# Attention with layernorm: x turned by 32x32 blocks on VectorE in place of TensorE transposes

## The chip, the cores and the metric

One core of one Trainium2 chip runs the whole kernel. The time is that of the device in microseconds (us), lower is better.

## The reference

x is (16, 30, 30, 512) in float32: 16 images of S = 900 tokens with 512 features. Everything is float32; each image goes through 8 heads of 64:

```python
q, k, v = proj(wq, bq), proj(wk, bk), proj(wv, bv)          # (B, 8, 900, 64)
scores = einsum('bhqd,bhkd->bhqk', q, k) / sqrt(64) + bias   # bias by |dh| + |dw| on the 30 x 30 grid
ctx = einsum('bhqk,bhkd->bhqd', softmax(scores), v)
resid = ctx_as_tokens @ wo + bo + x
out = (resid - mean) * rsqrt(var + 1e-5) * gamma + beta
```

## The kernel before

**Units and slots.** An image's attention is 60 units: 4 pairs of heads by 15 units of two image rows of queries (60 queries, both heads; the keys in two halves lie on different partitions). The order of everything is written out by hand over the unit number u, and each engine runs its own `body(im, u)`. TensorE acts on even u alone. A slot (even u) on TensorE is: the scores of units u + 6 and u + 7 (L693, 32 matmuls), a part of the P·V product of one group of up to 4 units (L713, `PV_UNITS` at L44; 8 blocks, then 7), and background work in r_ps, two PSUM banks used in turn.

**Background work.** `SEQUENCE` (L82) lists the items: `piece` (p, j), a half of K or Q of pair p of heads (L610), `out` t, a tile of 120 tokens of the output projection of the image before (L653), `value` t, a tile of V (L628), and `xt` t. All but `xt` have KT = 4 steps of three matmuls (a float32 operand is split into a rounded high part and the rest, and three of the four products are added); an `xt` is one step. `room_at` (L90) says how many steps a slot may hold, and `place` (L105) fills the slots in sequence and gives each item the unit `EVICT` in which it leaves PSUM. It comes out as: out tiles leave at u = 5, 7, 7, 9, 13, 17, 19 and 23, `xt` steps stand in the slots 28, 30, 34, 36, 38, 40, 42 and 44, one value tile in each of 34 to 44, and 128 steps besides the eight `xt` steps in all.

**x of the next image.** `load_x` (L500) on SyncE's queue loads 120 tokens, a token per partition, into one of 4 slots of `tokens` (units in `LOAD_X`, L47, for the first four, then two units after an `xt`). `xt_tile` (L572) transposes it on TensorE, four 120x128 transposes into one bank (L585). `xt_hi` (L749) copies the bank rounded to float32r into `xt[:, 0]` on ScalarE (L752). `xt_lo` (L920) subtracts that from the bank on VectorE into `xt[:, 1]` (L924) and frees the bank. `piece` and `value_tile` (L593, L615) read both parts. The residual of the layernorm takes the same `tokens` slots (`load_residual`, L504).

**Softmax.** VectorE adds the bias and takes the row minimum (L939, `biased_scores(u + 6)`; it may begin when TensorE has written the unit's scores, and TensorE may write a unit's scores when VectorE is done with the unit two before). ScalarE takes the exponential with its sum (L809, u + 6). The two halves of the keys then exchange minimum and sum: `exchange` (L491) issues four DMAs of 1 KB on SyncE's queue (L497), GpSimd finds the difference (`leads`, L1033, line L1041), ScalarE its exponential (`ratios`, L817), GpSimd the weight (`totals`, L1043, line L1052), ScalarE scales the rows (`normalise`, L825, u + 2) and VectorE block-transposes them for P·V (`turn`, L944, line L952, unit u).

**Out tiles.** GpSimd splits the context (`split_context`, L1067 and L1069, units in `SPLIT_UNITS`) and adds bias to the residual (`add_bias`, L1079); VectorE adds, takes statistics and centres (`out_sum`, L955, lines L963 to L969) in the unit of `EVICT`, and scales two units later (`out_norm`, L972, line L977); SyncE stores. `keep_value` (L481) stores value tiles from ScalarE's copy, `load_values` reads them back.

Of the kernel before, what the change touches and what calls it, by code (L numbers as in the profile page):

```python
# [13 lines left out]
TT = 120  # L14
# [32 lines left out]
LOAD_X = [22, 22, 25, 28]  # L47
# [42 lines left out]
def room_at(u):  # L90

    if u in (2, 32):
        return 3
    if u == UNITS - 2:
        return 2
    if u == 30:
        return 2
    return 4 if u < 16 and u % 4 == 0 else 5


def steps(item):
    return 1 if item[0] in ("xt", "first_xt", "bv_wo") else KT


def place(items):  # L105

    at, ends, room, u = {}, {}, 0, 0
    for item in items:
# [8 lines left out]
        ends[item] = min(e + (1 if used <= 2 or item[0] in ("xt", "out") else 2), UNITS - 1)  # L117
# [5 lines left out]
XT_UNITS = [u for tile in range(NT) for u in STEPS for w in STEPS[u] if w[0] == xt(tile)]  # L123
# [148 lines left out]
def attention_layernorm(nc, x, wq, bq, wk, bk, wv, bv, wo, bo, gamma, beta, spatial_bias, out):  # L272
# [3 lines left out]
    with ExitStack() as ctx:  # L276
# [31 lines left out]
        tokens = sb("tokens", [TT, SLOTS, D])  # L308
# [86 lines left out]
        xt_hi_done = sem("xt_hi_done")  # L395
# [42 lines left out]
        def _(sp):  # L438
# [75 lines left out]
            def body(im, u):  # L514
# [18 lines left out]
                if not im.last:  # L533
                    for t in range(SLOTS):
# [30 lines left out]
        def _(pe):  # L565
# [6 lines left out]
            def xt_tile(im, t):  # L572

                use = (im.xt, t)
                bank = bank_of(use)
                bank_wait(im, use)
                if isinstance(im, Prologue):
# [569 lines left out]
```

## Time and profile before

| | us |
|---|---|
| median of 3 runs | 3302.53 (3301.56 to 3307.05) |
| the profiled execution, its own time | 3300.92 |
| its span, first to last instruction | 3299.0 |
| TensorE busy | 3141.2 |
| ScalarE busy | 2758.5 |
| VectorE busy | 2608.9 |
| GpSimd busy | 1413.7 |

The sum, below, is made against the profiled execution. Names in the rows: PE is TensorE, PEld its weight loads, DVE VectorE, ACT ScalarE, POOL GpSimd, SPq SyncE's queue; L610 is line 610 of the kernel; xN is a count. In a row of windows stand the stretch and its length in us, then busy us and instructions of each engine, the granted TensorE clock (1.00 is full speed), the mean busy share of the 16 DMA engines and GB/s. In a row of the groups by line stand names, shapes and count, then busy us and mean ns of one, then the idle time of the engine before them and what ended it.

### The profile page before, as it was taken

How to read it: one execution, taken by the hardware profiler on the slowest of the kernel's cores; microseconds unless marked ns; L12 is line 12 of the kernel's file. 1: busy time of each engine (PE TensorE's matmuls, PEld its weight loads, DVE VectorE, ACT ScalarE, POOL GpSimd, SP SyncE). 2: the span in 40 equal slices, each digit the busy share in tenths (PEclk: the TensorE clock that was granted, in tenths of full speed). 3: DMA queues.
4: the chain of work that ended last, by engine and by line, in shares of the span. 5: the costliest groups of instructions: out<-in, count | busy, mean ns of one | idle time of the engine just before them, and what ended most of it. 6: DMA issues, size and time to landing. Idle time of an engine off the chain costs nothing. (4 is left out here: it accounts for less than half of the span.)

```text
span 3299.0 us, 127110 instructions
## 1 busy us (share of the span) xinstructions
PE 3141.2 (95%) x52744; PEld 2127.7 (64%) x52744; DVE 2608.9 (79%) x5589; ACT 2758.5 (84%) x7015; POOL 1413.7 (43%) x3049
## 2 busy tenths in 40 slices
PE   2899999999999999999999999999999999999986
PEld 2566666666666666666666666666666666666654
DVE  2477978878797887979778797887979778797887
ACT  1698897988889898898988889898898988889784
POOL 0133536354262533526344262543526344262545
PEclk7999999999999999999999999999999999999999
DMA  5222322323223232322323223232322323223221
GB/s 159 62 78 72 96 72 73 99 61 96 83 78 90 68 95 70 95 71 73 99 60 95 83 79 90 66 93 73 96 70 74 99 60 96 84 78 90 66 74 27
DMA packets 317939, 267.44 MB, mean 81 GB/s; under 512 B 109913, under 2 KB 240985, under 8 KB 317361
## 3 DMA queue, kind: packets, MB, share of 16 engines
q1 hardware_dynamic: 172242, 130.32, 15.2%
q10 hardware_dynamic: 145120, 129.00, 13.3%
q8 instruction: 415, 6.80, 0.9%
q14 instruction: 162, 1.33, 0.1%
HBM read 193.73 MB, written 63.66 MB: 78 GB/s over the span
## 5 line engine op out<-in xcount | busy, mean ns | idle before, releaser
L939 DVE CUSTOM_DVE_ANT_0 prob<-s_ps,window 128x450 f32<-128x450 f32 x1920 | 1108.3, 613 | 458.9 <-PE s_ps L693 458.8
L809 ACT ACTIVATE prob<-prob,own 128x450 f32<-128x450 f32 x1920 | 1266.2, 663 | 161.0 <-DVE own L939 151.0
L825 ACT ACTIVATE prob<-prob,weight 128x450 f32<-128x450 f32 x1920 | 1173.3, 660 | 75.0 <-POOL weight L1052 75.0
L952 DVE STREAM_TRANSPOSE prob_t<-prob 128x960 f32<-128x960 f32 x960 | 1125.5, 1173 | 57.4 <-PE pv_ps L713 34.5
L713 PEld LDWEIGHTS pv_ps<-prob_t,values 64*64 64x64 f32 x30720 | 752.5, 133 | 379.3 <-issue 335.8
L693 PE MATMUL s_ps<-k_sb,q_sb 64*32 64x450 f32 x15360 | 845.9, 544 | 43.8 <-DVE own L939 42.1
L713 PE MATMUL pv_ps<-prob_t,values 64*64 64x120 f32 x30720 | 856.2, 260 | 26.3 <-ACT ctx_sb L835 24.2
L610 PE MATMUL r_ps<-xt,w_sb 128*128 128x450 f32 x3072 | 705.8, 377 | 9.0 <-ACT stage L783 3.9
L610 PEld LDWEIGHTS r_ps<-xt,w_sb 128*128 128x128 f32 x3072 | 562.1, 189 | 94.7 <-issue 29.4
L1038 POOL TENSOR_TENSOR lead<-own,other 128x4 f32<-128x4 f32 x480 | 112.1, 233 | 1017.2 <-DMA other<-own 1016.8
L1052 POOL TENSOR_TENSOR weight<-total,minus_one 128x4 f32<-128x4 f32 x480 | 503.0, 1048 | 37.7
L693 PEld LDWEIGHTS s_ps<-k_sb,q_sb 64*32 64x32 f32 x15360 | 227.8, 106 | 436.8 <-issue 333.5
L628 PE MATMUL r_ps<-wv_sb,xt 128*120 128x512 f32 (+1 forms) x1536 | 391.5, 402 | 41.9 <-DVE wv_sb L908 38.6
L653 PE MATMUL r_ps<-wo_sb,ctx_split 128*120 128x512 f32 x1536 | 396.6, 403 | 4.6 <-POOL ctx_split L1069 3.3
L1047 POOL TENSOR_TENSOR total<-ratio,other 128x4 f32<-128x4 f32 x480 | 106.0, 221 | 661.2 <-ACT ratio L817 633.0
L809 ACT ACTIVATION_READ_ACCUMULATOR prob<-prob,own 128x1 f32 x1920 | 365.8, 191 | 0.0
L628 PEld LDWEIGHTS r_ps<-wv_sb,xt 128*120 128x120 f32 (+1 forms) x1536 | 261.1, 176 | 120.8 <-issue 41.3
L653 PEld LDWEIGHTS r_ps<-wo_sb,ctx_split 128*120 128x120 f32 x1536 | 271.3, 182 | 84.9 <-issue 17.6
L1079 POOL TENSOR_TENSOR tokens<-tokens,bo_all 120x512 f32<-120x512 f32 x120 | 156.3, 1308 | 56.9 <-DMA tokens<-in_x 56.9
L939 DVE DVE_READ_ACCUMULATOR2_ANT own<- 128x1 f32 x1920 | 157.3, 82 | 0.0
L1069 POOL TENSOR_TENSOR ctx_split<-ctx_sb,ctx_split 128x480 fp32r<-128x480 f32 (+1 forms) x128 | 149.9, 1171 | 10.3
L817 ACT ACTIVATE ratio<-lead 128x4 f32<-128x4 f32 x480 | 94.7, 197 | 67.5 <-POOL lead L1041 65.0
(56 smaller groups left out, 1462.7 us busy)
## 6 DMA issues: line engine op xcount, KB each, us to landing
w_sb<-w_split ACTq DMA_DIRECT2D x126, 512.0 KB, 4.0
values<-v_dram ACTq DMA_DIRECT2D x256, 240.0 KB, 3.2
tokens<-in_x SPq DMA_DIRECT2D x214, 240.0 KB, 3.2
other<-own SPq DMA_DIRECT2D x1920, 1.0 KB, 2.2
out<-tokens SPq DMA_DIRECT2D x105, 240.0 KB, 2.7
v_dram<-stage SPq DMA_DIRECT2D x96, 240.0 KB, 2.8
v_dram<-stage SPq DMA_DIRECT2D x32, 180.0 KB, 2.4
tokens<-in_x SPq DMA_DIRECT2D x30, 120.0 KB, 3.4
```

The lines of the kernel that those rows point to most:

```text
L610: last = pe.matmul(r_ps[:, bank, 0:HALF], w_sb[:, kind, a, k, :], xt[:, c, k, columns(half)], start=(k == 0 and i == 0), stop=(k == KT - 1 ...
L628: last = pe.matmul(r_ps[0:n, bank, :], xt[:, a, k, at:at + n], wv_sb[:, c, k, :], start=(k == 0 and i == 0), stop=(k == KT - 1 and i == PA ...
L653: last = pe.matmul(r_ps[0:TT, bank, :], ctx_split[:, t % 2, a, k, :], wo_sb[:, c, k, :], start=(k == 0 and i == 0), stop=(k == PAIRS - 1 a ...
L693: last = pe.matmul(s_ps[row:row + QUAD, u % 2, head, 0:HALF], q_sb[d, p % 2, q0:q0 + QUAD], k_sb[d, p % 2, columns(r)], start=True, stop=T ...
L713: last = pe.matmul(pv_ps[d, a, 0:n * GRID].rearrange("d (u w) -> d u w", u=n), values[half, p % 2, j, d], prob_t[half, g % 2, 0:n, head, Q ...
L809: nc.scalar.activation(prob[:, im.unit(u) % RING, head, 0:HALF], prob[:, im.unit(u) % RING, head, 0:HALF], ACT.Exp, scale=-1.0, bias=own[: ...
L825: nc.scalar.activation(prob[:, im.unit(u) % RING, head, 0:HALF], prob[:, im.unit(u) % RING, head, 0:HALF], ACT.Copy, scale=weight[:, s, c: ...
L939: nc.vector.tensor_tensor_reduce(prob[:, im.unit(u) % RING, head, 0:HALF], s_ps[:, u % 2, head, 0:HALF], window[:, w0:w0 + HALF // GRID, : ...
L952: nc.vector.transpose(out=prob_t[:, g % 2, v % PER_GROUP, :, :].rearrange("p h k -> p (h k)"), in_=prob[:, im.unit(u) % RING, :, :].rearra ...
L1052: nc.gpsimd.tensor_tensor(weight[:, s, :], total[:, s, :], minus_one[:, :], ALU.pow).then_inc(weight_done, 1)
L1069: nc.gpsimd.tensor_tensor(ctx_split[:, t % 2, 1, :, 0:m], src, ctx_split[:, t % 2, 0, :, 0:m].bitcast(F32), ALU.subtract).then_inc(split_l ...
L1079: nc.gpsimd.tensor_tensor(y, y, bo_all[0:rows(t), :], ALU.add).then_inc(res_bias, 1)
```

## The change

x of the next image is loaded in tiles of 128 tokens (`X_TILES` = 8, the last of 4 tokens), by four DMAs each, one for every 32 features of each group of 128. Each puts 32 tokens on 32 partitions, so that VectorE's block transpose of the whole tile (`turn_x`) gives features on partitions and tokens along the row. ScalarE writes the rounded part into `xt` (`x_split_hi`) and GpSimd the rest (`x_split_lo`). The `xt` items leave `SEQUENCE`, `room_at` is written anew, and value tiles and pieces wait for GpSimd's `x_lo`. The first image still passes TensorE. By the planner the out tiles now leave at u = 5, 7, 9, 11, 13, 17, 21 and 25; the slots 4 to 16 hold 4, 4, 4, 5, 4, 5, 4 steps (before 4, 5, 4, 5, 4, 5, 5), 24 to 34 hold 4, 5, 4, 4, 3, 5, and 36 to 44 a value tile each. `X_UNITS` is 31, 33, 35, 37, 39, 41, 43, 44.

```diff
-LOAD_X = [22, 22, 25, 28]
+LOAD_X = [22, 24, 28, 32]
...
-SEQUENCE += [xt(0), xt(1)]
-for tile in range(NT - 2):
-    SEQUENCE += [value(tile), xt(tile + 2)]
-SEQUENCE += [value(NT - 2)] + pieces(4) + [value(NT - 1)] + pieces(5, (0, 1, 2))
+SEQUENCE += [value(tile) for tile in range(NT - 1)] + pieces(4) + [value(NT - 1)] + pieces(5, (0, 1, 2))
...
 def room_at(u):
-    if u in (2, 32):
+    if u in (2, 32, UNITS - 2):
         return 3
-    if u == UNITS - 2:
-        return 2
-    if u == 30:
-        return 2
-    return 4 if u < 16 and u % 4 == 0 else 5
+    return 5 if u in (10, 14, 18, 22, 26, 34, 46, 48, 50, 52, 54) else 4
...
+VALUE_UNITS = [min(u for u in STEPS for w in STEPS[u] if w[0] == value(tile)) for tile in range(NT)]
+X_UNITS = [u - 1 for u in VALUE_UNITS[:NT - 1]]
+X_UNITS += [X_UNITS[-1] + 1]
...
+        x_turned = sb("x_turned", [128, 2, D])
...
             def load_x(b, t):
-                sp.dma_start(x_nat[0:rows(t), t % SLOTS, :], x_t[b, t * TT:t * TT + rows(t), :]
-                             ).then_inc(x_in[t % SLOTS], 16)
+                n = x_rows(t)
+                blocks, m = -(-n // QUAD), min(QUAD, n)
+                for a in range(128 // QUAD):
+                    part = bass.AP(tensor=x.tensor, offset=x.offset + (b * S + XB * t) * D + QUAD * a,
+                                   ap=[[D, m], [128, KT], [QUAD * D, blocks], [1, QUAD]])
+                    sp.dma_start(x_nat[QUAD * a:QUAD * a + m, t % SLOTS, 0:KT * blocks * QUAD].rearrange(
+                        "p (k b c) -> p k b c", k=KT, b=blocks), part).then_inc(x_in[t % SLOTS], 16)
...
-                        if u == XT_UNITS[t] + 2:
-                            use = ("xt", t)
-                            sp.wait_ge(bank_full[bank_of(use)], im.use(use) + 1)
+                        if u == X_UNITS[t]:
+                            sp.wait_ge(x_turn, X_TILES * im.b + t + 1)
                             load_x(im.b + 1, t + SLOTS)
...
+                    if j == 0 and p == PAIRS and im is not pro:
+                        pe.wait_ge(x_lo, X_TILES * (im.b + 1))
...
-                        xt_ready(im, t)
+                        pe.wait_ge(x_lo, X_TILES * im.b + x_tiles_to(at + n))
...
+            def x_split_hi(im, t):
+                n, m = X_TILES * im.b + t, x_rows(t)
+                if t == 0:
+                    for use in pieces(PAIRS - 1, (2, 3)):
+                        act.wait_ge(bank_full[bank_of(use)], im.use(use) + 1)
+                act.wait_ge(x_turn, n + 1)
+                turned_x = x_turned[:, t % 2, 0:KT * QUAD * -(-m // QUAD)].rearrange("p (k t) -> p k t", k=KT)[:, :, 0:m]
+                nc.scalar.activation(xt[:, 0, :, XB * t:XB * t + m], turned_x, ACT.Copy).then_inc(x_hi, 1)
...
+                for t in range(X_TILES):
+                    if X_UNITS[t] == u and not im.last:
+                        x_split_hi(im, t)
...
+            def turn_x(im, t):
+                n, width = X_TILES * im.b + t, KT * QUAD * -(-x_rows(t) // QUAD)
+                dve.wait_ge(x_in[t % SLOTS], 64 * (X_TILES // SLOTS * im.b + t // SLOTS + 1))
+                if n >= 2:
+                    dve.wait_ge(x_lo, n - 1)
+                nc.vector.transpose(out=x_turned[:, t % 2, 0:width], in_=x_nat[:, t % SLOTS, 0:width]).then_inc(x_turn, 1)
...
+                for t in range(X_TILES):
+                    if X_UNITS[t] - 2 == u and not im.last:
+                        turn_x(im, t)
...
+            def x_split_lo(im, t):
+                n, m = X_TILES * im.b + t, x_rows(t)
+                turned_x = x_turned[:, t % 2, 0:KT * QUAD * -(-m // QUAD)].rearrange("p (k t) -> p k t", k=KT)[:, :, 0:m]
+                pool.wait_ge(x_hi, n + 1)
+                nc.gpsimd.tensor_tensor(xt[:, 1, :, XB * t:XB * t + m], turned_x,
+                                        xt[:, 0, :, XB * t:XB * t + m].bitcast(F32), ALU.subtract).then_inc(x_lo, 1)
...
+                for t in range(X_TILES):
+                    if X_UNITS[t] == u and not im.last:
+                        x_split_lo(im, t)
```

`x_split_hi` stands in ScalarE's body behind the evictions and ahead of the exponentials, `turn_x` behind `turn` in VectorE's, `x_split_lo` in GpSimd's behind `totals` or `leads` and `reciprocal_std`.

## Rows read from the trace of the kernel before

**Rows 1.** The page: span; busy time, share and instructions of each engine.
```profile
span 3299.0 us, 127110 instructions
...
PE 3141.2 (95%) x52744; PEld 2127.7 (64%) x52744; DVE 2608.9 (79%) x5589; ACT 2758.5 (84%) x7015; POOL 1413.7 (43%) x3049
```

**Rows 2.** Windows, image 7, slots u = 4, 6, 10, 12, 24, 28, 30, 38, 58.
```profile
1507.62:1514.17 6.55, 6.53 (x109) 4.26 (x108) 5.42 (x12) 6.55 (x19) 4.21 (x8) 1.00 0.09 27
1514.17:1521.10 6.93, 6.93 (x104) 4.57 (x104) 6.83 (x15) 5.44 (x16) 6.53 (x12) 1.00 0.15 40
...
1527.54:1534.96 7.42, 6.84 (x104) 4.52 (x103) 7.32 (x17) 4.62 (x13) 6.25 (x13) 1.00 0.26 69
1534.96:1542.87 7.91, 6.67 (x110) 4.13 (x109) 7.91 (x17) 6.54 (x19) 4.34 (x6) 1.00 0.21 65
1576.22:1582.96 6.74, 6.74 (x112) 4.87 (x111) 6.17 (x14) 5.87 (x17) 2.96 (x7) 1.00 0.54 146
1589.49:1596.04 6.55, 6.55 (x113) 4.79 (x112) 4.43 (x10) 4.19 (x10) 1.86 (x5) 1.00 0.42 117
1596.04:1601.07 5.03, 4.59 (x96) 2.76 (x96) 3.30 (x7) 4.92 (x14) 1.43 (x3) 1.00 0.57 154
...
1621.25:1628.03 6.78, 6.78 (x113) 4.32 (x112) 5.09 (x11) 6.66 (x19) 2.07 (x6) 1.00 0.42 113
...
1689.03:1693.91 4.88, 4.88 (x103) 3.18 (x102) 3.79 (x10) 4.88 (x14) 1.42 (x3) 1.00 0.55 163
```

**Rows 3.** Timeline of VectorE in those slots: start, us, engine, line, operation.
```profile
1508.72 0.63 DVE L939 CUSTOM_DVE_ANT_0 prob<-s_ps,window 128x450 f32<-128x450 f32 x1 [1.42 <-PE s_ps L693]
...
1511.98 1.17 DVE L952 STREAM_TRANSPOSE prob_t<-prob 128x960 f32<-128x960 f32 x1
1513.08 0.65 DVE L963 TENSOR_TENSOR tokens<-r_ps,tokens 120x512 f32<-120x512 f32 x1
...
1515.41 0.61 DVE L939 CUSTOM_DVE_ANT_0 prob<-s_ps,window 128x450 f32<-128x450 f32 x1
...
1521.39 1.41 DVE L969 SCALAR_TENSOR_TENSOR tokens<-tokens,mean_var,gamma_all 120x512 f32<-120x512 f32 x1
...
1525.05 0.74 DVE L977 SCALAR_TENSOR_TENSOR tokens<-tokens,rstd,beta_all 120x512 f32<-120x512 f32 x1
1525.71 0.62 DVE L939 CUSTOM_DVE_ANT_0 prob<-s_ps,window 128x450 f32<-128x450 f32 x1
```

**Rows 4.** Timeline of TensorE: its waits in u = 10 and u = 12.
```profile
1529.11 0.99 PE L693 MATMUL s_ps<-k_sb,q_sb 64*32 64x450 f32 x16 [0.58 <-DVE own L939]
...
1537.08 0.99 PE L693 MATMUL s_ps<-k_sb,q_sb 64*32 64x450 f32 x16 [1.14 <-DVE own L939]
```

**Rows 5.** Groups of instructions by line, whole run.
```profile
L952 DVE STREAM_TRANSPOSE prob_t<-prob 128x960 f32<-128x960 f32 x960 | 1125.5, 1173 | 57.4 <-PE pv_ps L713 34.5 <-ACT prob L825 22.8
...
L1069 POOL TENSOR_TENSOR ctx_split<-ctx_sb,ctx_split 128x480 fp32r<-128x480 f32 (+1 forms) x128 | 149.9, 1171 | 10.3
...
L924 DVE TENSOR_TENSOR xt<-r_ps,xt 128x480 fp32r<-128x480 f32 (+1 forms) x128 | 77.6, 608 | 49.0 <-ACT xt L752 48.6
...
L752 ACT ACTIVATE xt<-r_ps 128x480 fp32r<-128x480 f32 (+1 forms) x128 | 67.5, 528 | 38.0 <-PE r_ps L585 38.0
...
L747 ACT ACTIVATE w_sb<-prob 128x512 fp32r<-128x512 f32 x2 | 1.3, 630 | 13.8 <-DMA prob<-in_L_conv_wq 9.4 <-DMA prob<-in_L_conv_wk 4.4
```

**Rows 6.** Waits, 1600 to 1800 us: us in total, times, longest us.
```profile
ACT ratio L817 <- POOL lead L1041: 3.1, 5, 1.1
...
PE r_ps L585 <- ACT q_sb L765: 0.9, 2, 0.4
```

**Rows 7.** DMA queues, 44 to 56 us, only the copy into `bias_by_w` under way.
```profile
q1 hardware_dynamic: 758, 0.09, 10.5%
```

**Rows 8.** Source view of the exchange's DMAs, L497.
```profile
DMA to landing us min/median/max: 1.6/2.2/4.5
```

**Rows 9.** Timeline of SyncE: four DMAs of one exchange.
```profile
1598.05 2.42 SPq L497 DMA_DIRECT2D other<-own  x4
```

More of the change, by code:

```diff
@@ L116, in place @@
         e = u - 2
-        ends[item] = min(e + (1 if used <= 2 or item[0] in ("xt", "out") else 2), UNITS - 1)
+        ends[item] = min(e + (1 if used <= 2 or item[0] == "out" else 2), UNITS - 1)
     assert max(at) < UNITS
@@ L122 @@
 STEPS, EVICT = place(SEQUENCE)
-XT_UNITS = [u for tile in range(NT) for u in STEPS for w in STEPS[u] if w[0] == xt(tile)]
+XB = 128
+X_BLOCKS = XB // QUAD
+X_TILES = -(-S // XB)
+VALUE_UNITS = [min(u for u in STEPS for w in STEPS[u] if w[0] == value(tile)) for tile in range(NT)]
+X_UNITS = [u - 1 for u in VALUE_UNITS[:NT - 1]]
+X_UNITS += [X_UNITS[-1] + 1]
+assert X_UNITS[0] > max(u for u in STEPS for w in STEPS[u] if w[0] == ("piece", PAIRS - 1, 3))
 BANK = {item: n % 2 for n, item in enumerate(SEQUENCE)}
@@ L142, in wanted @@
         return not first
-    if item[0] in ("xt", "value") or item[0] == "piece" and item[1] >= PAIRS:
+    if item[0] == "value" or item[0] == "piece" and item[1] >= PAIRS:
         return not last
@@ L260, in rows, with x_rows, x_tiles_to @@
     return LAST if t == NT - 1 else TT
+def x_rows(t):
+    return min(XB, S - XB * t)
+def x_tiles_to(token):
+    return -(-token // XB)
 def value_rows(t):
@@ L394, in attention_layernorm @@
         bank_free = [sem(f"bank_free{i}") for i in range(BANKS)]
-        xt_hi_done = sem("xt_hi_done")
+        first_hi = sem("first_hi")
+        x_turn = sem("x_turn")
+        x_hi = sem("x_hi")
+        x_lo = sem("x_lo")
         first_x_in = [sem(f"first_x_in{t}") for t in range(NT)]
@@ L570, in bank_wait, with first_xt @@
                     pe.wait_ge(bank_free[bank], n)
[L572 to L577, printed above, removed]
-                    tile = first_x(t)
-                    pe.wait_ge(first_x_in[t], 16)
-                else:
-                    tile = x_nat[:, t % SLOTS, :]
-                    pe.wait_ge(x_in[t % SLOTS], 16 * (NT // SLOTS * im.b + t // SLOTS + 1))
-                n = rows(t) if isinstance(im, Prologue) else TT
+            def first_xt(t):
+                use = ("first_xt", t)
+                bank, tile, n = bank_of(use), first_x(t), rows(t)
+                bank_wait(pro, use)
+                pe.wait_ge(first_x_in[t], 16)
                 for k in range(KT):
@@ L658, in work_on @@
             def work_on(im, work, k0=0, k1=KT):
-                if work[0] in ("xt", "first_xt"):
-                    xt_tile(im, work[1])
+                if work[0] == "first_xt":
+                    first_xt(work[1])
                 elif work[0] == "piece":
@@ L747, in weight_hi, with first_hi_of @@
                 nc.scalar.activation(dst, src, ACT.Copy, scale=scale).then_inc(w_hi, 1)
-            def xt_hi(im, t):
-                m, bank = rows(t), bank_of((im.xt, t))
-                act.wait_ge(bank_full[bank], im.use((im.xt, t)) + 1)
+            def first_hi_of(t):
+                m, bank = rows(t), bank_of(("first_xt", t))
+                act.wait_ge(bank_full[bank], pro.use(("first_xt", t)) + 1)
                 nc.scalar.activation(xt[:, 0, :, t * TT:t * TT + m],
                                      r_ps[:, bank, 0:KT * TT].rearrange("p (k t) -> p k t", k=KT)[:, :, 0:m],
-                                     ACT.Copy).then_inc(xt_hi_done, 1)
+                                     ACT.Copy).then_inc(first_hi, 1)
+            def x_split_hi(im, t):
[6 more added lines that the diff above has]
+                nc.scalar.activation(xt[:, 0, :, XB * t:XB * t + m], turned_x, ACT.Copy).then_inc(x_hi, 1)
             def keep_piece(im, p, j):
@@ L843, in _ @@
             for t in range(NT):
-                xt_hi(pro, t)
+                first_hi_of(t)
             weight_hi(wk_split[:, 0], raw_wk)
@@ L856, in body @@
                 for work in im.evicted(u):
-                    if work[0] == "xt":
-                        xt_hi(im, work[1])
-                    elif work[0] == "piece":
+                    if work[0] == "piece":
                         keep_piece(im, *work[1:])
@@ L1012, in body @@
                 for work in im.evicted(u):
-                    if work[0] == "xt":
-                        xt_lo(im, work[1])
-                    elif work[0] in ("out", "final"):
+                    if work[0] in ("out", "final"):
                         out_sum(im, work)
```

33 lines of the change are left out of this document (14 added, 19 removed).

## The prediction

> **What bounds the kernel now.** I read the page's engine table first: over the span TensorE is busy 95%, more than any other engine [rows 1]. A mean over stages settles nothing, so I then cut one middle image, b = 7, where the scores of a new pair of units start on TensorE (the even u of the plan). Each stretch is then one slot of the hand-written order: scores of two units, one part of a P·V group, 2 to 5 background steps. In the slots u = 24, 28, 38 and 58 TensorE's busy time equals the stretch and its clock is 1.00, that is 2.4 GHz [rows 2]: there the time is TensorE's own work. Two places differ. In u = 10 and 12 TensorE is idle 0.6 and 1.2 us while VectorE is busy for 7.32 of 7.42 and all of 7.91 us: the stage where the output tiles of the image before are normalised is VectorE's. In u = 30 TensorE is idle 0.44 us. ScalarE is a close second in the value stage: 6.66 of 6.78 us in u = 38 [rows 2].
>
> **TensorE: what goes.** Eight slots per image hold an `xt` step of four transposes. Slots alike in their P·V part (8 blocks of 4 units) price the steps: u = 24 has five piece steps in 6.74 us, u = 58 two in 4.88, so a piece step is 0.62; u = 28 has four and an `xt` in 6.55, so the `xt` is 6.55 - 6.74 + 0.62 = 0.43. u = 4 (four out steps, 6.55) gives 0.62 + 0.43 / 4 = 0.73 for an out step, u = 38 (four value steps and an `xt`, 6.78) 0.68 for a value step; scores and 8 blocks are 4.88 - 1.24 = 3.64. All 128 other steps stay, so 8 x 0.43 = **3.4 us per image** goes from the engine that sets the pace, provided no other wait takes the place.
>
> **The new order of the out tiles.** Rooms of 4 in place of 5 move the DVE evictions from u = 5, 7, 7, 9, 13 to 5, 7, 9, 11, 13. VectorE's own times: it starts a slot's body 1.10 us after TensorE's (1507.62 to 1508.72), two units' scores and turns take 4.36 (1508.72 to 1513.08), an out tile 2.33 (1513.08 to 1515.41), and its last operation, two units later, 0.66 (1525.05 to 1525.71) [rows 2, 3]. TensorE's second unit of scores starts 0.9 us into a slot (16 matmuls take 0.99 to their modelled end [rows 4]), but needs VectorE to be 3.27 us into the body before (1508.72 to 1511.98). With two tiles in one body this fails: the waits on VectorE of 0.58 and 1.14 us are that [rows 4], and the two slots together stand 7.42 + 7.91 - 6.5 - 6.45 = 2.4 us above what their steps come to by the prices above. After, counted from the start of u = 4: TensorE's slots start at 6.5, 12.7, 19.3, 25.8, 32.4, 38.9 (3.64 for scores and 8 P·V blocks, 3.3 with 7 by u = 6, plus steps). VectorE takes 4.36 + 2.33 + 0.66 = 7.35 per body and starts them at 7.8, 15.1, 22.5, 29.8, 37.2. It falls behind 1 us per slot, and first holds TensorE at u = 16: 37.2 + 3.27 = 40.5 against 38.9 + 0.9 = 39.8, a wait of 0.7. Some of its SCALAR_TENSOR_TENSORs are stretched, 1.41 us at 1521.39 against 0.74 at 1525.05 [rows 3]; at 0.3 us more per tile the same sum gives 1.9. I take 1.2, so of the 2.4 **1.1 us per image**, rounded down, comes back here (bounds 0.4 and 1.6). After u = 16 the bodies hold at most one tile every second slot and VectorE catches up.
>
> The Trainium skill (SBUF — State Buffer, "SBUF: two separate sides") says that a VectorE operation with two SBUF inputs and a GpSimd operation take turns on a shared port pair, for a whole instruction. The stretched row agrees. By that rule, with GpSimd's work spread evenly over these slots, many more could be held; the third rival below has its price from rows.
>
> **u = 30.** TensorE's idle 0.44 us and waits of 0.9 us per image at the transposes for ScalarE's bank [rows 2, 6] fall with the step; its slot is filled with four pieces (5.9 us). I take **0.5** (bounds 0 and 0.7).
>
> **ScalarE.** Eight copies from PSUM of 528 ns become seven of 128x512 from SBUF and a small one; the nearest row is 630 ns [rows 5], so 7 x 0.63 + 0.2 - 8 x 0.53 = +0.4 us per image. In the value slots its demand stays about 6.4 to 6.6 where TensorE's falls to 6.2 to 6.4 (7.0 in u = 34, which gets five steps). So the two tie. ScalarE works ahead: VectorE waited for its scaled rows 22.8 us in 960 turns [rows 5]. The copy of block 0 also waits for piece (3, 3), to the end of u = 30.
>
> **VectorE.** Eight subtracts of 608 ns become seven block transposes of 512 columns. 960 columns take 1173 ns [rows 5]; 512 lie between 0.63 (in proportion) and 0.75 (with 0.2 us fixed). 4.9 us out, 4.6 to 5.5 in: nothing, hidden by VectorE being busy only 5.1 of 6.8 us in these slots [rows 2]. Without that cover it would cost at most 0.6 us. x block 3 is the tight one: SyncE issues it at u = 32 behind block 4 and an exchange, for a turn at u = 35; I count a landing 0 to 1 us late, inside the 3 us that VectorE may lag before TensorE notices.
>
> **GpSimd.** The subtract of 128x480 takes 1171 ns [rows 5], so 128x512 some 1.25, seven times, 9 us per image beside 2.1 busy of 6.8 [rows 2]. It stands in odd bodies between `leads` and `totals`. ScalarE meanwhile runs two exponentials of 0.66 and the ratio, so `totals` is late by 0 to 1 us and the first scaling with it. A value tile needs the low part only a slot later.
>
> **DMA and SyncE.** Eight loads of 2 KB rows become 32 DMAs of 128 B runs, 14,400 packets per image. The nearest row is the prologue's copy of 120 B runs: 758 packets in 12 us at 10.5% of 16 engines, 0.105 x 16 x 12 / 758 = 26.6 ns of an engine each [rows 7]. A block of 2048 is 3.4 us of all 16 beside the latency, 24 us per image: some 12% more share. The loads are waited for 3 to 7 units after issue. What matters is who stands behind them: `exchange` uses the same queue, lands in 1.6 to 4.5 us, median 2.2 [rows 8], and the ratio already waits at times for what it feeds, 3.1 us in 200 [rows 6]. Four exchanges occupy SyncE 2.42 us [rows 9], 0.6 each, so a block's four loads 1.3 to 2.4. In odd units the exchange goes first and the next is two units off, so I charge the exchange, the late `totals` and ScalarE's tie together **0.4 us per image** (bounds 0 and 3).
>
> The skill (DMA: Bandwidth & Descriptors, "Rules for kernel authors") warns against many small transfers, mostly overhead under 64 KB; each new DMA has just 64 KB. By it the fourfold count is itself a price. That is the fourth rival's ground, and the trace has no load of this kind into SBUF.
>
> **Sum.** 3.4 + 1.1 + 0.5 - 0.4 = 4.6 us per image, 15 images with a next one to load (and 15 with out tiles): 69 us. The profiled execution took 3300.9 (a span of 3299.0 [rows 1] and 1.9 around it), which gives 3231.9; the median of the runs shown is 1.6 higher, so **3234 us**.
>
> **Rivals.**
> 1. ScalarE takes over in the value stage. For it: 6.66 busy of 6.78. Then the six `xt` steps of u = 34 to 44 are worth nothing (2.6 us) and the gain is 2.0 x 15 = 30 us: 3272. Against it: the lead it has. 0.14.
> 2. More than I sum: VectorE's stage runs with the wait of 0.7, nothing is charged for the chain, and u = 30 gives all: 3.4 + 1.6 + 0.7 = 5.7, 86 us, 3216. 0.20.
> 3. Port turns: if both SCALAR_TENSOR_TENSORs of each tile are held 0.6 us, a body is 8.5 us, starts are 16.3, 24.9, 33.4, 42, and TensorE waits about 5 us in place of 2.4. Gain 3.4 + 0.5 - 2.6 - 0.4 = 0.9, 13 us: 3289. Against it: GpSimd is busy 6.53 and 6.25 us in u = 6 and 10 already [rows 2], and the bodies there come to little over the sum of unstretched parts. 0.06.
> 4. Slower: the exchange. If the block loads push each of the eight exchanges near them to the 4.5 us landing, 2.3 later, and SyncE's longer issue adds 0.7, and the ratio has 1 us to spare, ScalarE stands 2 us eight times, 16 us, of which its lead takes some 9: 7 us against the 5.0 of the gains, so 2.0 x 15 = +30 us, 3332. It decides from 0.6 us per exchange on. For it: packet count and shared queue; against: the order in SyncE. 0.09.
> 5. The freed time only changes its name, TensorE waiting for `xt`'s low part where it transposed: 3302, 0.03.
>
> My forecast has 0.48. The range 3210 to 3280 takes in it, rival 1 and most of rival 2. A difference of 0.2% (6.6 us) is about what a measurement can tell. Faster 0.88 (the forecast and rivals 1 to 3), same 0.03, slower 0.09.
>
> **What would show it.** The transposes of L585 are left for the first image alone; slots u = 36 and 40 take 6.0 to 6.2 us and 38 and 42 near 6.4, with TensorE never idle (if ScalarE is busy all the slot and TensorE idle, rival 1). Waits of TensorE for VectorE's `own` near u = 14 and 16 only, about 1 us. The x transpose at 0.63 to 0.75 us. Landing of the exchanges still 2.2 in the median and ScalarE's wait for `lead` under 10 us in 200; more would be rival 4. TensorE waiting for GpSimd's low part of `xt` more than 0.5 us per image would prove my slack wrong.

## The result, and the profile after

| | before | after |
|---|---|---|
| median of 20 runs each, us | 3301.86 (3298.03 to 3307.05) | 3295.17 (3282.03 to 3301.57) |
| ratio, 95% interval | | 0.9976 (0.9968 to 0.9984) |
| span of the profiled execution | 3299.0 | 3295.8 |
| TensorE busy | 3141.2 | 3110.7 |

The kernel is faster by 0.24%, 6.7 us. The forecast was 3234 us with a range from 3210 to 3280, so it was wrong: about nine tenths of the expected gain is missing. This is the page after, its span, its engine table and the first DMA queue; the first two answer to [rows 1]:

```profile
span 3295.8 us, 126643 instructions
...
PE 3110.7 (94%) x52264; PEld 2090.6 (63%) x52264; DVE 2613.4 (79%) x5589; ACT 2760.8 (84%) x7015; POOL 1553.7 (47%) x3169
...
q1 hardware_dynamic: 379902, 130.34, 18.0%
```

TensorE has 30.5 us less work and the span is only 3.2 us shorter: TensorE now waits where it did not. To find where, I added up the slots of all middle images (1 to 13) from the timeline of TensorE, each from one start of scores to the next. Means per image in us, by stretches of the plan:

| slots u | before | after | one DMA per tile (below) |
|---|---|---|---|
| 0 to 2 | 12.46 | 12.44 | 12.45 |
| 4 to 14 | 42.34 | 40.83 | 40.60 |
| 16 to 28 | 46.49 | 45.09 | 45.11 |
| 30, 32 | 11.81 | 12.37 | 12.37 |
| 34 to 44 | 40.25 | **42.67** | 38.71 |
| 46 to 54 | 32.86 | 32.86 | 32.86 |
| 56, 58 | 11.74 | 11.66 | 11.69 |
| sum | 197.96 | 197.92 | 193.78 |

Some steps have also moved between stretches: by the planner u = 4 to 14 hold 26 steps and no longer 27, u = 16 to 28 hold 31 (before 34), u = 30 and 32 hold 7 (before 4), and u = 34 to 44 hold 25 (before 24), so a stretch alone does not give the worth of one part of the change. Up to u = 32 the image gains 2.4 us; the value stage, u = 34 to 44, takes back the same 2.4, and stands 4.0 above what it takes with one DMA per tile. Two slots do it: u = 36 is 7.25 in the mean and u = 40 is 8.86, both widely scattered (standard deviations of 1.3 and 1.6 us), where the last column has 6.23 and 6.24. These are u = 36, 38, 40 and 42 of image 7 after, in the view of windows (busy us and count of each engine, TensorE's clock, DMA share, GB/s):

```profile
1612.11:1619.40 7.29, 6.28 (x101) 4.02 (x100) 5.63 (x12) 5.33 (x14) 3.04 (x6) 1.00 0.37 71
1619.40:1625.80 6.40, 6.40 (x110) 3.93 (x109) 5.03 (x11) 3.48 (x10) 3.10 (x6) 1.00 0.57 120
1625.80:1635.87 10.07, 7.45 (x102) 4.65 (x101) 5.20 (x11) 9.15 (x23) 3.54 (x8) 0.87 0.27 65
1635.87:1642.68 6.81, 6.81 (x109) 4.25 (x108) 4.63 (x11) 6.69 (x18) 2.72 (x4) 0.94 0.31 94
```

TensorE idles 1.0 us in u = 36 and 2.6 in u = 40. In u = 38 nothing is lost on TensorE, but ScalarE is busy for only 3.48 of 6.40 us, in a stage that should keep it full: its stop there is what TensorE pays for a slot later. The waits of TensorE in the whole profiled execution, after (line waited for: us, times, longest), and the groups of the lines that stand between SyncE and it (the first three with the shapes kept apart, so without the 15 short tiles of 4 tokens):

```profile
PE r_ps L632 <- POOL xt L1101: 43.6, 27, 3.6
...
PE s_ps L697 <- DVE own L962: 31.8, 51, 1.5
```

```profile
L950 DVE STREAM_TRANSPOSE x_turned<-tokens 128x512 f32<-128x512 f32 x105 | 71.0, 676 | 22.9 <-DMA tokens<-in_x 22.9
...
L768 ACT ACTIVATE xt<-x_turned 128x512 fp32r<-128x512 f32 x105 | 65.0, 619 | 8.6 <-issue 6.6
...
L1101 POOL TENSOR_TENSOR xt<-x_turned,xt 128x512 fp32r<-128x512 f32 x105 | 134.6, 1282 | 57.4 <-ACT xt L768 56.8
...
L797 ACT ACTIVATE stage<-r_ps 120x512 f32<-120x512 f32 (+1 forms) x128 | 74.3, 580 | 57.0 <-DMA v_dram<-stage 47.7 <-PE r_ps L632 9.1 <-ACT stage L797 0.2
...
L831 ACT ACTIVATE ratio<-lead 128x4 f32<-128x4 f32 x480 | 94.5, 197 | 109.2 <-POOL lead L1065 108.0
```

The last two in the kernel before:

```profile
L783 ACT ACTIVATE stage<-r_ps 120x512 f32<-120x512 f32 (+1 forms) x128 | 74.4, 582 | 15.5 <-PE r_ps L628 15.3 <-ACT stage L783 0.2
...
L817 ACT ACTIVATE ratio<-lead 128x4 f32<-128x4 f32 x480 | 94.7, 197 | 67.5 <-POOL lead L1041 65.0
```

TensorE's value tile (L632) waits 43.6 us for GpSimd's rest of x, 2.9 per image. The engines on the way wait as well: VectorE's block transpose 22.9 us for its load, GpSimd 56.8 for ScalarE's rounded part (this one is no sign by itself: with one DMA per tile, below, it is still 44.1 and TensorE does not wait), and ScalarE 47.7 us for a **store**, `v_dram<-stage`, the transfer out of its own staging buffer. That wait was not there in the kernel before: the same group (L783) waited 15.5 us, 15.3 of it for TensorE. The ratio's wait for `lead` went from 65.0 to 108.0. The durations themselves are near what was expected: 676 ns for a whole tile's block transpose, 619 for its rounded part, 1282 for its rest.

Loads, stores and exchanges have one thing in common, SyncE's queue. Its timeline in the same image (start, duration, line, names, how many in a row):

```profile
1600.91 3.13 SPq L501 DMA_DIRECT2D other<-own  x4
1604.09 6.72 SPq L511 DMA_DIRECT2D tokens<-in_x  x8
1610.86 2.53 SPq L501 DMA_DIRECT2D other<-own  x4
1613.43 2.67 SPq L511 DMA_DIRECT2D tokens<-in_x  x4
1616.14 2.53 SPq L501 DMA_DIRECT2D other<-own  x4
1618.72 2.67 SPq L511 DMA_DIRECT2D tokens<-in_x  x4
1621.49 0.56 SPq L493 DMA_DIRECT2D v_dram<-stage  x1
1622.10 3.44 SPq L501 DMA_DIRECT2D other<-own  x4
1625.65 0.52 SPq L493 DMA_DIRECT2D v_dram<-stage  x1
1626.21 2.76 SPq L511 DMA_DIRECT2D tokens<-in_x  x4
```

From 1604.09 to 1629 the queue has no gap over 0.11 us. There are two jams in it. **First**, tile 4 (u = 31) and tile 3 (u = 32) stand back to back, eight DMAs, 6.72 us; the exchange behind them starts at 1610.86, 3.8 us after the exponentials that it waits for had ended on ScalarE (1607.09). In the mean of the images 1 to 13 this exchange, of unit 38, goes out 3.0 us late and the next 2.4, where the kernel before has 0.0 for both. **Second**, the loads of the next tile (1618.72) stand ahead of the store at 1621.49, for whose landing ScalarE's next copy into that buffer waits. The other end of both, GpSimd and ScalarE in the same stretch:

```profile
1614.56 0.20 POOL L1062 TENSOR_TENSOR lead<-own,other 128x4 f32<-128x4 f32 x1 [5.71 <-DMA other<-own]
...
1615.04 1.27 POOL L1101 TENSOR_TENSOR xt<-x_turned,xt 128x512 fp32r<-128x512 f32 x1
...
1630.34 1.27 POOL L1101 TENSOR_TENSOR xt<-x_turned,xt 128x512 fp32r<-128x512 f32 x1 [2.62 <-ACT xt L768]
```

```profile
1626.48 0.60 ACT L797 ACTIVATE stage<-r_ps 120x512 f32<-120x512 f32 x1 [3.60 <-DMA v_dram<-stage]
...
1629.64 0.61 ACT L768 ACTIVATE xt<-x_turned 128x512 fp32r<-128x512 f32 x1
```

```profile
1616.46 3.02 PE L632 MATMUL r_ps<-wv_sb,xt 128*120 128x512 f32 x12 [1.01 <-POOL xt L1101]
...
1631.75 4.18 PE L632 MATMUL r_ps<-wv_sb,xt 128*120 128x512 f32 x12 [2.62 <-POOL xt L1101]
```

GpSimd's subtract stands behind `lead` in its program. `lead` waits 5.71 us for the late exchange, the subtract ends at 1616.31, and TensorE starts 1.01 us late. In the second jam ScalarE stands 3.60 us for the store, its rounded part starts at 1629.64, GpSimd's rest at 1630.34, and TensorE goes on 2.62 us late. That value tile then takes 4.18 us where the one before took 3.02, with the granted clock at 0.87 in the mean of the slot, so partly at 1.2 in place of 2.4 GHz: here the wait costs 1.2 us more after it has ended (7.45 busy, against 6.24 in the same slot without the wait, shown below).

Two theories stood at this point. **A**: SyncE's issue time, four DMAs of 0.64 us in place of one of 0.55, holds exchanges and stores. **B**: the 128 B runs themselves (379,902 packets on the queue, 172,242 in the kernel before) slow what lands beside them. Further suspects were GpSimd's long subtract, the place of the single loads, and the new order of the out tiles.

### The profile page after: what moved, and what is told of

It reads as the page before. It is cut to its first block and busy times, and to the rows that moved or that the text cites. A ratio compares the mean times of both kernels' runs of the same rounds, so it can differ in the third digit from the quotient of the medians.

```text
span 3295.8 us, 126643 instructions
## 1 busy us (share of the span) xinstructions
PE 3110.7 (94%) x52264; PEld 2090.6 (63%) x52264; DVE 2613.4 (79%) x5589; ACT 2760.8 (84%) x7015; POOL 1553.7 (47%) x3169
## 3 DMA queue, kind: packets, MB, share of 16 engines
q1 hardware_dynamic: 379902, 130.34, 18.0%
## 5 line engine op out<-in xcount | busy, mean ns | idle before, releaser
L697 PE MATMUL s_ps<-k_sb,q_sb 64*32 64x450 f32 x15360 | 850.1, 544 | 35.7 <-DVE own L962 31.8
L1062 POOL TENSOR_TENSOR lead<-own,other 128x4 f32<-128x4 f32 x480 | 101.7, 212 | 1098.2 <-DMA other<-own 1097.9
L632 PE MATMUL r_ps<-wv_sb,xt 128*120 128x512 f32 (+1 forms) x1536 | 400.7, 412 | 82.9 <-POOL xt L1101 43.6
L632 PEld LDWEIGHTS r_ps<-wv_sb,xt 128*120 128x120 f32 (+1 forms) x1536 | 270.8, 182 | 180.4 <-issue 100.6
L831 ACT ACTIVATE ratio<-lead 128x4 f32<-128x4 f32 x480 | 94.5, 197 | 109.2 <-POOL lead L1065 108.0
L1101 POOL TENSOR_TENSOR xt<-x_turned,xt 128x512 fp32r<-128x512 f32 x120 | 137.9, 1150 | 62.0 <-ACT xt L768 61.4
```

The source lines that it names most:

```text
L632: last = pe.matmul(r_ps[0:n, bank, :], xt[:, a, k, at:at + n], wv_sb[:, c, k, :], start=(k == 0 and i == 0), stop=(k == KT - 1 and i == PA ...
L697: last = pe.matmul(s_ps[row:row + QUAD, u % 2, head, 0:HALF], q_sb[d, p % 2, q0:q0 + QUAD], k_sb[d, p % 2, columns(r)], start=True, stop=T ...
L1101: nc.gpsimd.tensor_tensor(xt[:, 1, :, XB * t:XB * t + m], turned_x, xt[:, 0, :, XB * t:XB * t + m].bitcast(F32), ALU.subtract).then_inc(x_ ...
```

## The experiments

Every ratio is to the kernel before; a difference in us to the changed kernel is to its 3295.2.

### The same runs in one DMA, and plain rows

```diff
-                for a in range(128 // QUAD):
-                    part = bass.AP(tensor=x.tensor, offset=x.offset + (b * S + XB * t) * D + QUAD * a,
-                                   ap=[[D, m], [128, KT], [QUAD * D, blocks], [1, QUAD]])
...
+                token = XB * t if n < QUAD else min(XB * t, S - 224)
+                part = bass.AP(tensor=x.tensor, offset=x.offset + (b * S + token) * D,
+                               ap=[[D, m], [128, KT], [QUAD * D, blocks], [1, QUAD]])
```

> The changed kernel, but each x tile of 128 tokens is fetched by one DMA of 128 partitions with the same 2048 runs of 128 B, in place of four of 32 partitions. The parts of x land in other places than needed, so the sum of products is of other numbers; work and bytes are the same. Theory A (SyncE's issues: four loads of 0.67 us at each of u = 31, 32, 33, 35 and 37 push the exchange and the stores of the value tiles back): the slots u = 34 to 44 fall from 42.7 us per image to 39 to 39.5, and the time to 3235 to 3250. Theory B (the packets: 128 B runs slow the queue and the exchange): all packets are still there, so the time stays at 3290 to 3300. Theory C (GpSimd's subtract stands before the totals, ScalarE is the bound of the value slots): no change either, 3290 to 3300, and issue-to-exponential delays stay.

Measured: **3232.57 us, ratio 0.9797 (0.9782 to 0.9811)**. The packets stay (373,962 on the queue), the count of DMAs per tile falls from four to one of 0.68 us, and 63 us come off. Its groups:

```profile
L797 ACT ACTIVATE stage<-r_ps 120x512 f32<-120x512 f32 (+1 forms) x128 | 74.3, 580 | 18.4 <-DMA v_dram<-stage 9.5 <-PE r_ps L632 8.6 <-ACT stage L797 0.2
...
L950 DVE STREAM_TRANSPOSE x_turned<-tokens 128x512 f32<-128x512 f32 x120 | 74.6, 622 | 2.1 <-DMA tokens<-in_x 2.1
```

The wait for the store falls from 47.7 to 9.5, that of the transpose from 22.9 to 2.1, TensorE's for the rest of x is gone, and no exchange of the stage goes out late (0.0 in the mean for units 36 to 44).

```diff
+                m = x_rows(t)
+                width = D if m == 128 else KT * QUAD
+                sp.dma_start(x_nat[0:m, t % SLOTS, 0:width], x_t[b, XB * t:XB * t + m, 0:width]).then_inc(x_in[t % SLOTS], 16)
```

> The changed kernel with each x tile fetched by one DMA of 128 rows of 2 KB (the layout for the block transpose is left out, so values and pieces are made of x in another order). Neither four issues nor short runs. Theory A: the same time as with one DMA of 128 B runs, 3235 to 3250. Theory B: clearly faster than that one, by its 26.6 ns x 14,400 packets of engine time or more, and the first of the two that leaves 3290. Theory C: 3290 to 3300 still.

Measured: 3235.34 us, 0.9804 (0.979 to 0.9819). Sixteen times fewer packets per tile make no difference in time to the kernel with 128 B runs in one DMA, so B falls as the cause. The short runs do slow a neighbour a little: the store of the first value tile, which stands right behind a load, lands 4.2 us after its issue in the one kernel and 3.2 in the other (means over 15 images, by the trace; 4.4 in the changed kernel). ScalarE waits 9.5 us in all for that store in the one kernel and not at all in the other, and TensorE for it in neither.

### Four DMAs again, with runs of 512 B; and rows with three or five small DMAs

```diff
-                                   ap=[[D, m], [128, KT], [QUAD * D, blocks], [1, QUAD]])
+                                   ap=[[D, m], [QUAD * D, blocks], [1, 128]])
```

> The changed kernel with each of a tile's four DMAs fetching 4 runs of 512 B per partition (128 neighbouring features) in place of 16 runs of 128 B; same bytes, places and count of DMAs, a quarter of the packets (the order of the features in xt is then another than the weights', so the result is of other products). Theory A, an issue costs the same however long its runs: 3288 to 3300. If the issue time hangs on the pattern (three dimensions in place of four) and falls from 0.64 to near 0.35, as for the row loads: 3240 to 3260. Theory B: 3240 to 3260 too, but with issues still of 0.64 us.

Measured: 3239.4 us, 0.981 (0.9794 to 0.9827). This looks like B at first, since the count of DMAs stays and the packets fall. But the issue times moved too, as the view of one line shows (min/median/max ns):

```profile
L511 SPq DMA_DIRECT2D tokens<-in_x x480: 288/432/1903, 187.9 to 2957.4; - x160
```

In the changed kernel, the same line:

```profile
L511 SPq DMA_DIRECT2D tokens<-in_x x480: 583/637/1964, 189.0 to 3017.1; - x160
```

So a tile costs SyncE 1.7 us here and 2.5 to 2.8 there. To hold the two apart, the next two kernels load rows and add small DMAs of 1 KB each that only take up the queue.

```diff
+                for a in range(3):
+                    sp.dma_start(spare[:, t % SLOTS, 8 * a:8 * a + 8], x_t[b, QUAD * a:QUAD * a + QUAD, 0:8]).then_inc(x_in[t % SLOTS], 16)
```

> The version with one DMA of 2 KB rows per tile (3235 us), plus three DMAs per tile of 32 partitions x 32 B into a buffer that nobody reads: the issues come back, the bytes and short runs do not (96 packets a tile). The layout for the block transpose is left out as there. Theory A (SyncE's issue time alone): some 0.6 us each, 24 more per image at the same places, so the slots 34 to 44 go back to 42 to 43 us and the time to 3285 to 3300. Theory B (packets, DMA share): stays within 5 us of 3235.

Measured: 3238.67 us, 0.9805 (0.9791 to 0.982), against my expectation. The reason is in the issue times, which I had not measured for so small a DMA:

```profile
L511 SPq DMA_DIRECT2D spare<-in_x x360: 310/422/2238, 189.7 to 2958.0; - x180
```

Three at 0.42 and the rows at 0.58 are 1.8 us per tile: the count of four was back, SyncE's time was not. With five small ones:

> As the version with 2 KB rows and three small DMAs per tile (3239 us, where a tile took SyncE 0.58 + 1.36 = 1.9 us and not the 2.7 of the changed kernel: the small ones cost 0.42 each), but with five small ones: 0.58 + 5 x 0.45 = 2.8 us per tile. Nothing else of the changed kernel's loads is there (160 tiny runs a tile, one load of rows). Theory A, SyncE's time per tile at these places is the cause, whatever it is spent on: slots 34 to 44 back to 42 to 43.5 us, time 3285 to 3305. Rival: it takes the 128 B runs and four issues together (theory B in a mixed form): within 10 us of 3239.

Measured: **3295.73 us, 0.9983 (0.9972 to 0.9995)**: 0.58 + 5 x 0.42 = 2.7 us per tile, rows of 2 KB, and the whole loss is back. Its timeline of SyncE has the same first jam, now of twelve DMAs, and its groups the same waits:

```profile
1606.10 0.58 SPq L509 DMA_DIRECT2D tokens<-in_x  x1
1606.72 2.28 SPq L511 DMA_DIRECT2D spare<-in_x  x5
1609.05 0.42 SPq L509 DMA_DIRECT2D tokens<-in_x  x1
1609.52 3.08 SPq L511 DMA_DIRECT2D spare<-in_x  x5
1612.64 2.41 SPq L502 DMA_DIRECT2D other<-own  x4
```

```profile
L796 ACT ACTIVATE stage<-r_ps 120x512 f32<-120x512 f32 (+1 forms) x128 | 74.4, 581 | 49.5 <-DMA v_dram<-stage 40.2 <-PE r_ps L631 9.2 <-ACT stage L796 0.2
```

A is shown: SyncE's time per tile decides, whatever the DMAs carry. The exchanges of units 38 and 40 are late again too, by 3.6 and 3.3 us in the mean. The dose is sharp: 1.8 us per tile costs 3 to 6 us in all against one DMA (3238.7 to 3235.3 and 3232.6, about what the measurement can tell), 2.7 costs 60.

### Which jam: tile 3 earlier, the store first, both

```diff
-LOAD_X = [22, 24, 28, 32]
+LOAD_X = [22, 24, 28, 30]
```

> The changed kernel with the load of x tile 3 issued at u = 30 in place of u = 32, nothing else; the result is whole. In the trace SyncE idles some 4 us there, while at u = 31 and 32 eight loads in a row take 6.72 us and the next exchange is issued 3.1 us after its exponential. Theory A: the exchange of unit 38 goes out within 0.5 us of its exponential, the slots 34 to 44 lose 1.5 to 3 us per image, time 3250 to 3275. Theories B and C: same packets, same subtract, no change, 3290 to 3300.

Measured: 3266.55 us, 0.9897 (0.9883 to 0.9912), 29 us under the changed kernel. Slot 36 is whole again (6.23 in the mean over images), slot 40 is not (7.93). The exchange of unit 38 is not within the 0.5 us of the expectation, it is still 1.1 us late in the mean (3.0 in the changed kernel). ScalarE still waits for the store:

```profile
L797 ACT ACTIVATE stage<-r_ps 120x512 f32<-120x512 f32 (+1 forms) x128 | 74.3, 580 | 51.4 <-DMA v_dram<-stage 43.1 <-PE r_ps L632 8.1 <-ACT stage L797 0.2
```

The other jam alone: tiles 4 to 7 are issued at u = 31, 33, 36 and 38, so that tiles 6 and 7 follow the stores of their slots, and tile 3 stays at 32.

```diff
+MORE_X = [31, 33, 36, 38]
...
-                        if u == X_UNITS[t]:
+                        if u == MORE_X[t]:
```

> The changed kernel with tiles 6 and 7 loaded at u = 36 and 38, behind the stores of value tiles, and tile 3 left at u = 32 behind tile 4. It splits the gain of the version with all three moved (3235.5) from the other side: tile 3 alone gave 29 us (3266.5). If the two jams are separate, the store's share is the other 31 us and this stands at 3262 to 3270. If the late exchange of unit 38 feeds the later one, this wins little: 3275 to 3290.

Measured: 3252.68 us, 0.9857 (0.9842 to 0.9872), 42 us under. Slot 40 falls to 6.59, slot 36 stays at 7.42. ScalarE's wait for the store is gone (1.4), while the exchanges of units 38 and 40 stay 3.4 and 2.8 us late and VectorE still waits for its load:

```profile
L798 ACT ACTIVATE stage<-r_ps 120x512 f32<-120x512 f32 (+1 forms) x128 | 74.2, 580 | 12.7 <-PE r_ps L633 11.1 <-DMA v_dram<-stage 1.4 <-ACT stage L798 0.2
...
L951 DVE STREAM_TRANSPOSE x_turned<-tokens 128x512 f32<-128x512 f32 x120 | 75.3, 627 | 28.2 <-DMA tokens<-in_x 26.4 <-POOL xt L1102 1.8
```

Both edits together, with all four 128 B loads per tile as in the change:

> The changed kernel, result whole, with only the places of its loads moved: tile 3 at u = 30 (was 32), tile 6 at u = 36 behind the store of the first value tile (was 35, ahead of it), tile 7 at 38 (was 37). Theory A: what is left of the loss with tile 3 moved alone (slot 40 at 7.9 us) is the store of a value tile that stands behind four loads, while ScalarE needs its staging buffer; with the store first, slot 40 falls to 6.3 to 6.8 and the time to 3235 to 3250. Theory B or C: 3260 to 3270 as with tile 3 alone.

Measured: **3235.51 us, 0.9798 (0.9777 to 0.9819)**. The change itself is worth 66 us, once two lists of units say when its loads are issued. It beats both kernels. The slots u = 36, 38, 40 and 42 of image 7 in this kernel, and SyncE in the first two of them:

```profile
1587.62:1593.84 6.22, 6.22 (x101) 4.02 (x100) 5.03 (x11) 6.10 (x16) 3.45 (x8) 1.00 0.57 115
1593.84:1600.24 6.40, 6.40 (x110) 3.93 (x109) 5.03 (x11) 6.28 (x17) 2.72 (x4) 1.00 0.49 91
1600.24:1606.48 6.24, 6.24 (x102) 4.03 (x101) 5.03 (x11) 6.12 (x16) 3.25 (x7) 1.00 0.36 92
1606.48:1612.93 6.45, 6.45 (x109) 4.23 (x108) 4.63 (x11) 6.33 (x17) 2.97 (x6) 1.00 0.41 111
```

```profile
1589.30 2.46 SPq L502 DMA_DIRECT2D other<-own  x4
1591.87 0.52 SPq L494 DMA_DIRECT2D v_dram<-stage  x1
1592.43 2.69 SPq L512 DMA_DIRECT2D tokens<-in_x  x4
1595.74 3.41 SPq L502 DMA_DIRECT2D other<-own  x4
```

TensorE is busy for the whole of every slot, at full clock. SyncE is as full in u = 36 as in a slot of the changed kernel with a load and a store, 2.5 + 0.5 + 2.7 = 5.7 of 6.2 us, but nothing urgent stands behind a load. The two jams are not a plain sum: by the medians their removal alone gives 29 and 42 us, together 60; in the profiled executions it is 33, 37 and 65, so which jam is the larger is not clear. One thing that both share is seen in the traces: an image in which TensorE's granted clock fell below 0.95 in a slot of the stage occurs 9 times in 15 in the changed kernel, 2 times with tile 3 moved, once with the store first and never with both. Whether that is all of the overlap is not shown.

### GpSimd's subtract, and the order of the out tiles

With the loads spread, the subtract is moved to VectorE, in the same units:

```diff
-                nc.gpsimd.tensor_tensor(xt[:, 1, :, XB * t:XB * t + m], turned_x,
+                nc.vector.tensor_tensor(xt[:, 1, :, XB * t:XB * t + m], turned_x,
                                         xt[:, 0, :, XB * t:XB * t + m].bitcast(F32), ALU.subtract).then_inc(x_lo, 1)
```

> The version with the loads spread, and the subtract that makes the rest of x moved from GpSimd to VectorE, in the same units, result whole. If GpSimd's place between leads and totals costs anything (theory C), this is faster than the loads spread alone, by up to 0.5 us per image. If not, VectorE's 0.65 us and its wait for ScalarE's rounded part come on top in slots where it is idle 1.5 us or more: 0 to +15 us over the loads spread alone.

Measured: 3238.65 us, 0.9813 (0.9795 to 0.983), the same as with GpSimd within the spread (3229 to 3244 there, 3238 to 3248 here). With the loads spread, GpSimd's 1285 ns for a whole tile are hidden as well as VectorE's 685, and the place of the subtract costs nothing. In the changed kernel itself the subtract stands behind the late `lead` on GpSimd and carries the first jam to TensorE; whether another place would have spared it there was not run.

The new plan of u below 28 is taken back to that of before, with u = 28 at four steps and u = 30 empty:

```diff
 def room_at(u):
-    if u in (2, 32, UNITS - 2):
+    if u < 28:
+        return 3 if u == 2 else 4 if u < 16 and u % 4 == 0 else 5
+    if u == 28:
+        return 4
+    if u == 30:
+        return 0
+    if u in (32, UNITS - 2):
```

> The changed kernel with the slots below u = 28 filled as in the kernel before (out tiles leave at 5, 7, 7, 9, 13, 17, 19, 23), u = 28 with piece (3, 3) and u = 30 with no step; the value slots unchanged. My reading of the VectorE stage: u = 4 to 14 goes back from 40.8 to 42.3 us per image, u = 30 becomes a short slot of about 5 us and the total is 1 to 2 us per image longer, 3305 to 3325. Rival: the order of the out tiles is worth nothing, since VectorE catches up later anyway: within 5 us of 3295.

Measured: 3317.66 us, 1.005 (1.0033 to 1.0067), 22.5 us over the changed kernel. TensorE's waits for VectorE's scores in it:

```profile
PE s_ps L703 <- DVE own L968: 63.6, 59, 1.5
```

They are 63.6 us, against 31.8 with the new order and 42.1 before. That looks like a large gain of the new order, and it is not: this kernel changes a second thing, the empty u = 30. Summed by slot over the images 1 to 13, TensorE waits for VectorE's scores 2.05 us per image in u = 8 to 12 (before 2.13) and another 1.53 in u = 32, right behind the empty slot, as in image 7:

```profile
1608.88 0.99 PE L703 MATMUL s_ps<-k_sb,q_sb 64*32 64x450 f32 x16 [1.53 <-DVE own L968]
```

The slot u = 30 is over in 3.27 us, and VectorE has not taken the scores that TensorE must overwrite. 15 times 1.53 is 23 us, about all that this kernel loses (TensorE waits 0.3 us per image less for the rest of x in it, against 0.3 more for the order). My expectation for it came true in number (42.3 us in u = 4 to 14, 3305 to 3325), but of the 1.5 us more there 0.7 is a step that moved back into the stretch. The new order itself is worth the difference of the first sum: 2.05 here against 1.76 us in the changed kernel and 1.55 with the loads spread, 0.3 to 0.5 us per image or 4 to 8 us in all. A kernel with the old order and a full u = 30 was not run.

## Why the prediction was wrong

**The step that failed** is the price under "DMA and SyncE": "a block's four loads 1.3 to 2.4" us on SyncE, and with them "I charge the exchange, the late `totals` and ScalarE's tie together 0.4 us per image (bounds 0 and 3)". The term measured 197.92 - 193.78 = 4.1 us per image, above its upper bound of 3; over the 15 images with a next one to load that is 62 us, and the miss is 61. Three things went wrong in it.

- The size. I took the 0.6 us of an exchange DMA [rows 9] as the upper end. The 4-dimensional pattern takes 0.64, and four come to 2.67 to 2.76 us.
- What stands behind. I reasoned that "in odd units the exchange goes first and the next is two units off". That was never summed over the slot. An exchange of 2.5, a store of 0.5 and a tile of 2.7 fill 5.7 of 6.2 us, and tile 3 comes on top at u = 32. I had seen this ("SyncE issues it at u = 32 behind block 4 and an exchange") and gave it only "a landing 0 to 1 us late" for its own reader; the exchange behind both, 3.0 us late in the mean, I did not price.
- A waiter left out. The stores of the value tiles (`keep_value`) are on the same queue, and ScalarE waits for them before it reuses its staging buffer. They stand in no line of the prediction, and putting two loads behind them gives 42 us alone.

**Rival 4** had the right queue and the wrong size and sign: it priced the landing of exchanges at 4.5. The landing hardly moved (median 2.2 as in [rows 8], longest 5.5); what grew was the time until an exchange was issued. Its mark, "ScalarE's wait for `lead` under 10 us in 200", held at 8.4 in the stretch from 1600 to 1800 and so did not warn; the mark that did was the last, TensorE waiting for the rest of x, 2.9 us per image against the 0.5 allowed.

The price of the packets was too high as well: the prologue's row gave 26.6 ns of an engine each and "some 12% more share", and the share rose by 2.8 points (15.2% to 18.0%), some 7 ns for each of the 207,660 further packets. It stood in no term of the sum.

**What held, and what was luck.** With the queue relieved the kernels measure 3232.6 to 3239.4, and the forecast was 3234. The terms without the 0.4 were 5.0 us per image, and 4.2 came (197.96 - 193.78). That these kernels stand so near 3234 is in part luck: they do not pay the 0.4 that the forecast charged, and that covers half of the 0.8 by which the other terms were too high. Term by term, from TensorE's timeline with one DMA per tile (means of images 1 to 13):

- The `xt` steps: forecast 3.4, and TensorE's busy time fell by 3.0 (194.83 to 191.84), so 0.37 a step for 0.43.
- The new order: forecast 1.1, and TensorE's waits for VectorE fell by 0.6 (2.13 to 1.54), inside the bounds of 0.4 and 1.6. What is left in image 7 of the changed kernel is 1.9 us, the end of my range (0.7 to 1.9): 0.22 in u = 12, 1.17 in u = 14 and 0.49 in u = 16, so the forecast's "near u = 14 and 16" was right but for the first.
- u = 30: forecast 0.5, and the wait of 0.44 is gone. The "0.9 us per image" beside it was a misreading: the row says 0.9 in two waits, and a stretch of 200 us holds this slot of two images, so it is the same 0.44.
- The slots: forecast 6.0 to 6.2 in u = 36 and 40, near 6.4 in u = 38 and 42; the spread kernel has 6.22, 6.24, 6.40 and 6.45. u = 30 takes 5.93, forecast 5.9.
- The durations of a whole tile, short ones left out: block transpose 676 ns (forecast 630 to 750), GpSimd's subtract 1282 (1250), ScalarE's rounded part 619 (630).
- Rivals 1 and 3 did not happen: with the queue relieved ScalarE is busy 6.10 to 6.33 us of 6.2 to 6.45 and still holds nobody in those slots, and the port turns left the stall at 1.9, not 5. That VectorE and GpSimd take turns is neither shown nor denied by that.

The Trainium skill (DMA: Bandwidth & Descriptors, "Rules for kernel authors") says to coalesce many small transfers into a large one. As the loads stood in the change, the trace agrees with the advice: one DMA of 256 KB in place of four of 64 KB is worth 63 us. It doesn't agree with overhead in the transfer as the reason. A tile by four DMAs is whole 6.1 us after its first issue and a tile by one 4.2 (medians of the tiles whose landings the profile has), and that difference is what the three further issues take on SyncE (3 x 0.67 = 2.0). With the loads at other units the four cost nothing. The same section advises to issue a load early and to wait for it late. For tile 3, two units earlier, the runs agree (29 us); for tiles 6 and 7 they say the opposite, a unit later and behind the stores is worth 42 us, since an early load holds what stands behind it on the queue.

## What to carry to other kernels

Before you split a transfer, add up the issue time of everything on that engine's queue over one period of the schedule, with the duration of that very kind of access pattern, and list who waits for each entry that stands behind the new ones, stores that free a buffer included. The queue here was 90% full, and it cost nothing once its urgent entries came first: moving three of eight loads by one or two units was worth 60 us. When a change moves little, compare slot by slot; a gain and a loss of the same size can hide in one mean. And when a run takes one part of a change back, look by slot whether it opened another hole: the kernel with the old order lost 22.5 us to an empty slot, not to the order.

## What was not expected of the hardware

- The issue time of a DMA on SyncE goes with its access pattern and not with bytes or packets in proportion (medians): 0.58 us for 128 rows of 2 KB, 0.42 for 1 KB in 32 runs, 0.43 for 64 KB in runs of 512 B, 0.64 for 64 KB in 512 runs of 128 B with four dimensions, and 0.68 for 256 KB in 2048 such runs. Four times the runs cost 0.04 us more. That the number of dimensions is what counts between 0.43 and 0.64 fits this, but no run holds it apart from the length of the runs.
- It also goes with what was issued just before. The same load of 120 rows of 2 KB in the kernel before took 0.33 us after a gap in the queue, 0.58 right behind an exchange and 0.41 right behind a store:

```profile
1595.18 0.33 SPq L501 DMA_DIRECT2D tokens<-in_x  x1
...
1600.51 0.58 SPq L501 DMA_DIRECT2D tokens<-in_x  x1
...
1618.77 0.41 SPq L501 DMA_DIRECT2D tokens<-in_x  x1
```

- 207,660 packets more, nearly all of them of 128 B, raised the queue's share from 15.2% to 18.0%. Runs of 128 B cost no time that the measurements can tell, though the store behind such a load lands 1 us later: with one DMA per tile 3232.6 us, with rows of 2 KB 3235.3.
- A stall can cost TensorE more than its length: 2.62 us of idle time in u = 40 was followed by a granted clock of 0.87 in that slot and 0.94 in the next, with 1.2 and 0.4 us more busy time than the spread kernel needs for the same matmuls. It is not so for every stall: in 9 of the 15 images a slot of the value stage had a clock of 0.83 to 0.87, in the other 6, with slots of up to 8.7 us, it stayed at 1.00. The mean granted clock of the execution is 0.984 after and 0.990 with the loads spread.
